# Another order for the same operations on all five engines of a macaron transformer block

## What is computed

```python
x = x + 0.5 * ffn(_layernorm(x), w_gate, w_up, w_down)
x = x + attn(_layernorm(x), Wq, bq, Wk, bk)
x = x + 0.5 * ffn(_layernorm(x), w_gate, w_up, w_down)
```

## Time and profile before

| | us |
|---|---|
| median of 3 runs (2418.31 to 2423.77) | 2418.92 |
| the profiled execution's own time | 2417.81 |
| its span, first to last instruction | 2416.0 |
| VectorE busy | 2067.1 |
| TensorE busy (matmul) | 2044.3 |
| ACT busy | 1697.1 |
| GpSimd busy | 1078.2 |

### The profile page before, as it was taken

The page is one execution under the profiler, slowest core; times in us unless marked ns, Lnnn a source line. Parts: engine busy times, 40 slices in busy tenths (PEclk is TensorE's granted clock), DMA queues, the critical chain, the costliest instruction groups (busy, mean ns, idle before and its releaser), DMA issues. The chain is left out here.

```text
span 2416.0 us, 45454 instructions
## 1 busy us (share of the span) xinstructions
PE 2044.3 (85%) x12746; PEld 1184.2 (49%) x12746; DVE 2067.1 (86%) x3833; ACT 1697.1 (70%) x4251; POOL 1078.2 (45%) x1111
## 2 busy tenths in 40 slices
PE   2577988988898888898889889889888988988876
PEld 1244555545555554554545555455554545555543
DVE  6567899889888888999989999898999989998865
ACT  3457777777777686787767778777876877787651
POOL 3134444544444353544444454444544544454431
PEclk6889999999999998999999999999999999999987
DMA  1233544454444455454445544444443444445432
GB/s 54 49 61 70 97 96 91 100 93 93 92 99 90 86 95 96 85 100 95 94 81 108 95 86 99 92 97 95 94 99 85 97 95 90 94 97 100 84 70 61
DMA packets 741632, 214.83 MB, mean 89 GB/s; under 512 B 706464, under 2 KB 741152, under 8 KB 741408
## 3 DMA queue, kind: packets, MB, share of 16 engines
q1 hardware_dynamic: 741408, 212.54, 44.2%
HBM read 19.53 MB, written 16.78 MB: 15 GB/s over the span
## 5 line engine op out<-in xcount | busy, mean ns | idle before, releaser
L1188 PE MATMUL gu_ps<-wgu_hi,xT 128*128 128x512 f16 (+1 forms) x3072 | 933.6, 368 | 64.9 <-DMA xT<-f_dq 44.5
L573 POOL TENSOR_TENSOR tile_area<-tile_area,h_rs 128x704 f32<-128x704 f32 x256 | 379.7, 1483 | 675.3 <-DVE h_rs L1009 675.3
L1188 PE MATMUL gu_ps<-wgu_lo,xT 128*128 128x512 f16 (+1 forms) x1536 | 564.9, 368 | 0.0
L1252 PE MATMUL out_ps<-wd_hi,hT 128*128 128x256 f16 x1536 | 382.6, 289 | 178.9 <-DMA hT<-h_dq 178.7
L1188 PEld LDWEIGHTS gu_ps<-wgu_hi,xT 128*128 128x128 f16 x3072 | 305.4, 99 | 398.8 <-issue 56.2
L1252 PE MATMUL out_ps<-wd_lo,hT 128*128 128x256 f16 (+1 forms) x1536 | 396.1, 290 | 0.0
L1051 DVE SCALAR_TENSOR_TENSOR tile_area<-gu_ps,gu_unit,tile_area 128x704 f32<-128x704 f32 x256 | 236.3, 923 | 85.6 <-ACT tile_area L890 44.7
L890 ACT ACTIVATE tile_area<-gu_ps,gu_unit 128x704 f32<-128x704 f32 x256 | 215.6, 842 | 129.6 <-PE gu_ps L1188 128.9
L1252 PEld LDWEIGHTS out_ps<-wd_hi,hT 128*128 128x128 f16 x1536 | 157.7, 103 | 248.6 <-issue 169.1
L720 ACT ACTIVATE h_y<-tile_area 128x704 bf16<-128x704 f32 x256 | 200.6, 784 | 84.1 <-POOL tile_area L573 82.4
L1188 PE MATMUL out_ps<-xs_hi,pT 128*128 128x256 f16 x1024 | 190.4, 274 | 63.2 <-DMA pT<-p 60.4
(11 more groups left out here) (168 smaller groups left out, 4247.4 us busy)
## 6 DMA issues: line engine op xcount, KB each, us to landing
x<-in_L_attn_x SPq DMA_DIRECT2D x32, 512.0 KB, 3.9
out<-x_later SPq DMA_DIRECT2D x32, 512.0 KB, 3.3
hT<-h_dq SPq DMA_TRANSPOSE x256, 3.6
pT<-p SPq DMA_TRANSPOSE x128, 2.8
xT<-f_dq SPq DMA_TRANSPOSE x64, 4.3
w_raw<-in_L_ffn_w_down SPq DMA_DIRECT2D x1, 704.0 KB, 6.8
w_raw<-in_L_ffn_w_gate SPq DMA_DIRECT2D x1, 640.0 KB, 4.4
w_raw<-in_L_ffn_w_up SPq DMA_DIRECT2D x1, 640.0 KB, 5.2
```

The source lines that it names most:

```text
L573: g.tensor_tensor(blocks(h_xq[:, n % 2, :], FB), blocks(hid[:, n % 2, :], FB), per_block(h_rs[:, n % 2, 0:FB], FB), ALU.mult).then_inc(xq_ ...
L1188: ins = t_.matmul(dst, x, y, start=(i == 0), stop=(i == len(todo) - 1))
L1252: ins = t_.matmul(out_bank(turn_down[n]), h, w, start=(i == 0), stop=(i == len(terms) - 1))
```

## The change

No operation is added, removed or resized. It is announced as another order on all five engines with the FFN's second product placed later in TensorE's program. In the diff TensorE's second product (`s.tile[4]`) keeps its lines and its age; the two projections of the attention, which stood ahead of it in the slot, go to age 3: the first behind the second gate product, the second (with the rho products) behind the third.

VectorE's order of tile steps in a slot becomes: h_q (age 2), h_rs (age 1), high product (age 2), hid, block maxima (age 0), low product (age 2), residual add (age 3), h_sl (age 1), the maximum of the block maxima (age 0), h_t (age 1), h_s (age 0). Both `qT_lo` stand around the low product, `s_mneg` behind hid, one attention residual add ahead of the low product and one behind it, `f_sl` ahead of the low product and the front's high product behind the residual add. On ACT `h_unit` ends a slot (age 1), the afront's last Squares go ahead of Silu, `h_s`-based `f_sh` to an earlier place, `qT_hi` of half 0 behind Silu, `xs_hi` between the two Exp. On GpSimd the quotient ends the slot (age 2), the first `prob` goes ahead of it, `a_ve`, `a_rstd` and `a_shift` go ahead of the quotient they followed. SyncE's blocks change places and ages. The core of the diff, for TensorE:

```diff
-A_TURNS = (("q0", "afront", 4), ("q1", "afront", 4))
+A_TURNS = (("q0", "afront", 3), ("q1", "afront", 3))
...
             def emit(s, pair):
-                if s.afront[4] is not None:
-                    b = s.afront[4]
...
-                    project(tr_a, 0).then_inc(a_full.sem, 1)
                 if s.query[5] is not None:
...
                     attend(a, 0, turn_att0[a]).then_inc(out_full.sem, 1)
-                if s.afront[4] is not None:
...
-                    project(tr_a, 1).then_inc(a_full.sem, 1)
                 if s.tile[4] is not None:
...
                     gate_up(n, 1).then_inc(gu_full.sem, 1)
+                if s.afront[3] is not None:
...
+                    project(tr_a, 0).then_inc(a_full.sem, 1)
                 if s.query[2] is not None:
...
                     gate_up(n, 2).then_inc(gu_full.sem, 1)
+                if s.afront[3] is not None:
...
+                    project(tr_a, 1).then_inc(a_full.sem, 1)
```

For VectorE:

```diff
             def emit(s, pair):
...
-                    dve.wait_ge(am_done.sem, am_done.at(n + 1, pair))
-                    v.tensor_reduce(h_am[:, n % 2, FB:FB + 1], h_am[:, n % 2, 0:FB], AX.X, ALU.max).then_inc(hm_done.sem, 1)
+                if s.query[4] is not None:
...
+                if s.afront[3] is not None:
+                    b = s.afront[3]
+                    dve.wait_ge(q_hi_done.sem, q_hi_done.at(DC * b + 1, pair))
+                    v.tensor_tensor(qT_lo[:, 0, :], qT[:, 0, :], qT_hi[:, 0, :], ALU.subtract).then_inc(ql_done.sem, 1)
+                if s.front[2] is not None:
...
+                if s.tile[2] is not None:
+                    n = s.tile[2]
+                    dve.wait_ge(sl_done.sem, sl_done.at(n + 1, pair))
+                    v.tensor_tensor(pairs(h_dq[:, n % 2, FF:2 * FF]), pairs(h_q[:, n % 2, :]),
+                                    per_pair(h_sl[:, n % 2, :, :], FB), ALU.mult).then_inc(dl_done.sem, 1)
...
+                if s.tile[1] is not None:
+                    n = s.tile[1]
+                    dve.wait_ge(sh_done.sem, sh_done.at(n + 1, pair))
...
+                if s.tile[0] is not None:
+                    n = s.tile[0]
+                    dve.wait_ge(am_done.sem, am_done.at(n + 1, pair))
+                    v.tensor_reduce(h_am[:, n % 2, FB:FB + 1], h_am[:, n % 2, 0:FB], AX.X, ALU.max).then_inc(hm_done.sem, 1)
```

For ACT, at the end of a slot:

```diff
             def emit(s, pair):
...
+                if s.tile[1] is not None:
+                    n = s.tile[1]
+                    act.wait_ge(rs_done.sem, rs_done.at(n + 1, pair))
...
+                    a_.activation(h_unit[:, n % 2:n % 2 + 1], h_rs[:, n % 2, FB:FB + 1], ACT.Copy, scale=-SH).then_inc(unit_done.sem, 1)
```

More of the change, by code:

```diff
@@ L539, in emit @@
                                            f_dq[:, :, :].rearrange("p h d -> p (h d)")).then_inc(xT_in[f % 2].sem, 16)
+                if s.query[2] is not None:
+                    turn_probs(s.query[2], 1, pair)
+                if s.afront[0] is not None:
+                    turn_tokens(s.afront[0], 0, pair)
                 if s.j == 3 and 0 <= s.it - 3 < SEQS:
@@ L609, in emit @@
                     g.tensor_tensor(f_shift[:, :], f_nm[:, :], f_rstd[:, :], ALU.mult).then_inc(f_shift_done.sem, 1)
+                if s.front[3] is not None:
+                    f = s.front[3]
+                    pool.wait_ge(f_rs_done.sem, f_rs_done.at(f + 1, pair))
+                    if pair is not None or f >= 1:
+                        pool.wait_ge(f_t_done.sem, f_t_done.at(f, pair))
+                    g.tensor_tensor(blocks(f_xq[:, :], XB), blocks(f_xn[:, :], XB),
+                                    per_block(f_rs[:, :], XB), ALU.mult).then_inc(f_xq_done.sem, 1)
                 if s.query[4] is not None:
@@ L794, in emit @@
                                   bias=s_nmean[:, 1:2]).then_inc(p_hi_done.sem, 1)
+                if s.front[1] is not None:
+                    f = s.front[1]
+                    ffn, seq = info["front"][f]
+                    src = x0 if ffn == 1 else x2
+                    for t in (2, 3):
+                        a_.activation(f_xn[:, t * D:(t + 1) * D], src[:, seq % 2, t, :], ACT.Identity, scale=f_rstd[:, t:t + 1],
+                                      bias=f_shift[:, t:t + 1]).then_inc(f_xn_done.sem, 1)
                 if s.afront[4] is not None:
@@ L829, in emit @@
-                if s.front[1] is not None:
-                    f = s.front[1]
-                    ffn, seq = info["front"][f]
-                    src = x0 if ffn == 1 else x2
-                    for t in (2, 3):
-                        a_.activation(f_xn[:, t * D:(t + 1) * D], src[:, seq % 2, t, :], ACT.Identity, scale=f_rstd[:, t:t + 1],
-                                      bias=f_shift[:, t:t + 1]).then_inc(f_xn_done.sem, 1)
+                        act.wait_ge(a_ve_done.sem, a_ve_done.at(b, pair))
@@ new lines, in emit @@
+                    for t in (0, 1):
+                        a_.activation(a_scrap2[:, t, :], x1[:, b % 2, t, :], ACT.Square, bias=a_nm[:, t:t + 1],
+                                      accum_out=a_ss[:, t:t + 1]).then_inc(a_ss_done.sem, 1)
+                if s.afront[3] is not None:
+                    b = s.afront[3]
+                    act.wait_ge(a_full.sem, a_full.at(turn_q0[b] + 1, pair))
+                    if pair is not None or b >= 1:
+                        act.wait_ge(ql_done.sem, ql_done.at(DC * (b - 1) + 1, pair))
+                    a_.activation(qT[:, 0, :], tr_a[:, :], ACT.Identity, scale=SQ / (SX * SM),
+                                  bias=c_col[:, 0:1]).then_inc(a_free.sem, 1)
@@ new lines, in emit @@
+                if s.tile[1] is not None:
+                    n = s.tile[1]
+                    dve.wait_ge(lifted.sem, lifted.at(n + 1, pair))
+                    v.scalar_tensor_tensor(out=h_t[:, n % 2, :], in0=h_y[:, n % 2, :], scalar=ROUND_MIN,
+                                           in1=h_xq[:, n % 2, :], op0=ALU.max, op1=ALU.add).then_inc(t_done.sem, 1)
+                if s.front[1] is not None:
+                    f = s.front[1]
+                    dve.wait_ge(f_lifted.sem, f_lifted.at(f + 1, pair))
+                    v.scalar_tensor_tensor(out=f_t[:, :], in0=f_y[:, :], scalar=ROUND_MIN, in1=f_xq[:, :],
+                                           op0=ALU.max, op1=ALU.add).then_inc(f_t_done.sem, 1)
@@ new lines, in emit @@
+                if s.front[2] is not None:
+                    f = s.front[2]
+                    dve.wait_ge(f_sl_done.sem, f_sl_done.at(f + 1, pair))
+                    v.tensor_tensor(pairs(f_dq[:, 1, :]), pairs(f_q[:, :]),
+                                    per_pair(f_sl[:, :, :], XB), ALU.mult).then_inc(f_dl_done.sem, 1)
+                if s.tile[0] is not None:
+                    n = s.tile[0]
+                    dve.wait_ge(hm_done.sem, hm_done.at(n + 1, pair))
+                    if pair is not None or n >= 2:
+                        dve.wait_ge(sigma_done.sem, sigma_done.at(n - 1, pair))
+                    v.tensor_scalar(h_s[:, n % 2, :], h_am[:, n % 2, :], 1.0 / 6.0, SMALL, ALU.mult,
+                                    ALU.max).then_inc(s_done.sem, 1)
@@ L1111, in _ @@
+                if s.query[2] is not None:
+                    a = s.query[2]
+                    dve.wait_ge(exp_done.sem, exp_done.at(2 * a + 2, pair))
+                    if pair is not None or a >= 1:
+                        dve.wait_ge(prob_done.sem, prob_done.at(2 * a, pair))
+                    v.reciprocal(s_rsum[:, :], s_sum[:, :]).then_inc(rsum_done.sem, 1)
             for u, (at, n) in enumerate(UNITS):
```

443 lines of the change are left out of this document (189 added, 254 removed).

## The result

The changed kernel takes 2494.98 us (median of 4 runs, 2490.39 to 2508.99) against 2418.61 for the kernel before beside it; the ratio is 1.0338, 95% interval 1.0302 to 1.0374. The direction was the forecast one (2442), the size three times as large: +76 us instead of +23, outside the range of 2402 to 2470. The profiled execution took 2496.04 us, 78.2 more than that of before.

A forecast was written before the change was run, and what follows sets the result against it. VectorE, busy 86%, was nearest to a bound, no engine full. Stretches A, C, D, E gave +32.7, F without a turn -17.6, with one +8.4: +23.5 on 2417.8, so 2442 us as median; range 2402 to 2470.

The forecast's parts named there:

- C: VectorE's stretch from slot 4's row maxima to slot 5's gate product (hid), 9.71 us: +0.11 for the tile's maximum.
- E: VectorE's stretch from hid(6) to hid(7), 7.21 us: +0.29, with two ACT Squares going ahead of slot 7's Silu.
- D: VectorE's stretch from hid(5) to hid(6), 9.03 us: +0.44, the low product being blocked until GpSimd's f_xq ends.
- A: VectorE's stretch from slot 0's block maxima to tile 0's low product in slot 2, 14.53 us: +0.25, largest term qT_lo blocked.
- F with a turn: Stretch from hid(7) to the next iteration's block maxima when the loop branches, 16.8 us: +0.6, 14 times.
- F without a turn: Stretch from hid(7) to the next iteration's block maxima without a loop branch, 14.61 us: -1.1, 16 times.
- B: Stretch from tile 0's low product in slot 2 to slot 4's row maxima, 13.58 us: 0, its hT chain unchanged.
- All turns become long: Rival: shifted branch fetches meet the hT transpose at every turn, +50 us, 2492; chance 0.13.
- Nothing moves: Rival: cycles nearly the same, second product not moved, blocks fall otherwise; 2418, no change; chance 0.15.
- cheap turn: Rival: VectorE does lift sum and scale under the fetch, ACT's fetch leaves the hT transpose free; 2398; chance 0.25.
- drain rule: Rival: drains happen regardless of neighbours, so three savings of 0.11 in A and C don't come; 2452; chance 0.05.

The follow-up runs named there:

- new_prob_back: The changed kernel with GpSimd's first `prob` moved back behind the tile's quotient; ratio 1.0152 (1.0091-1.0212) to the kernel before.

## Why the prediction was wrong

**What held.** The change's VectorE and TensorE orders alone cost nothing (0.9998, 0.9994). With the probability put back, C is 9.81 (forecast 9.71 + 0.11) and E 7.39 (7.50), as means of new_prob_back. The idle time ahead of hid(0) is gone, with a high product of 2.29 beside xs_lo, as forecast. D's mechanism is there too, a low product of slot 5 that takes 1.55 us beside f_xq, over the 1.2 that I named as its mark; but D is 9.10 against 9.04 before and not 9.47, and in the change itself the low product took only 0.79, so that mark did not show. A came to 14.65 in the iteration shown (forecast 14.78) and to 14.43 on average, 0.11 less than before, so its +0.25 did not come.

**First term that failed: C at +0.11, D at +0.44 and E at +0.29, without GpSimd's `prob`.** The prediction took GpSimd's blocks from f_xq, p_lo and xs_lo, and left the one that moves ahead of the quotient unpriced, though the change moved it. It measures 45 us (1.0338 to 1.0152). In the means, against new_prob_back: C 10.78 instead of 9.81, E 7.97 instead of 7.39 through TensorE's clock, and D 8.33 instead of 9.10, a gain.

**Second term that failed: the turn, +0.6 on F with bounds of -1.1 and +1.9.** The mechanism was named: ACT's later branch and VectorE's wait for Abs ahead of its own. Its size was taken as half covered. It isn't: the typical step 7 with a turn rose by 2.2 us, and F with a turn, the two more long ones included, by 3.2 (18.29 to 21.45). Putting both places back took 3.4 us off the typical turn (33 us over the 13 turns of the traces, from a mean of 14.15 to 11.59). The forecast set 0.9 of a hidden branch and an early Silu against it; VectorE's branch still shows 2.27 us, and behind it `h_q` takes 1.96.

**Third: F without a turn, -1.1.** It measures +0.03. hid(0) came 8.52 after hid(7) where 8.15 was said; and `f_xn` is not "ready sooner": ACT waits for `f_shift`, as `f_rstd` and `f_shift` on GpSimd take 1.40 and 0.73 us there. 16 iterations had been credited with 1.1 us each, 18 us.

**Fourth: B at nothing, since "the chain of B keeps its length".** In the iteration shown B is 13.27 rather than 13.58, and TensorE's wait for hT 1.48 us rather than 3.12. I had said that such a shrinking would prove me wrong, but the hT transpose did not get faster: TensorE starts on it 4.42 us after the low product starts, 4.55 before. The wait is 2.7 to 3.1 us in 16 iterations of the change and 1.5 in nine, in all of them up to 0.4 to 0.5 us ahead of hid(3), so in the nine it is the matmuls ahead of it that ended later. Over all iterations B rose by 0.67 us, 19 in all; 0.37 of it is step 3. In 10 of 28 iterations step 3 is 11.75 to 12.00 us, in the others 9.52 to 9.74; before, it was 11.3 to 11.6 in three, 9.93 to 10.20 in 19 and 9.03 in six. TensorE's timeline in a long iteration, and the windows of it and of the next:

```profile
1381.66 0.28 PE L1236 MATMUL out_ps<-wd_hi,hT 128*128 128x256 f16 x1 [2.78 <-DMA hT<-h_dq]
```

```profile
1382.10:1390.10 8.00, 7.48 (x28) 3.10 (x26) 6.94 (x12) 4.63 (x16) 5.70 (x6) 0.57 0.53 105
1459.30:1465.00 5.70, 4.47 (x28) 2.36 (x26) 5.67 (x10) 4.63 (x16) 4.37 (x5) 1.00 0.47 88
```

After 2.78 us of waiting for hT the clock is 0.57, and after 1.48 for hT and 1.23 for xT it stays at 1.00. In the 8 us behind hid(3) it is 0.57 in each of the ten long iterations and 1.00 in 16 of the others. The wait alone doesn't decide it, since in four of these 16 TensorE had waited 2.8 to 3.0 us too. Step 3 costs 0.37 us more on average than before, 10 us in all. No run isolates it. One part can be told: the shortest step 3 is 9.50 to 9.52 in every kernel with VectorE's new order and 9.03 in the kernel before, where TensorE has its xT 2.0 to 2.1 us behind hid(3) instead of 3.0.

**The rivals.** "All turns become long" gave 2492, close to the measured time, but for another reason: long turns rose from 4 to 6, not to 14. "Nothing moves" and "cheap turn" fell. "The second product isn't moved" held as a statement: TensorE's order alone is within 0.3%. The drain rule stays unsupported: in the change the block maxima and their next instruction, now independent, start 0.80 apart (1453.43 and 1454.22), 0.92 when it depended. The forecast's own range of 2428 to 2458 doesn't follow from its ends: 2442 less 24 and plus 18 is 2418 to 2460.

## What to carry to other kernels

When orders change, price every instruction that changes sides with another on every engine, the short ones on a shared port too: 0.77 us of GpSimd work ahead of a long operation moved that operation onto VectorE's path and cost some 45 us. Orders of different engines are one design: each new list alone cost up to 2.7%, and together less than the sum. Put an engine's loop branch where it would wait for another engine anyway, with all that others wait for already issued; with two engines' branches, see that neither waits for what stands behind the other's.
